# Gated cross-attention block with a mixture of experts: the dense second layer as three bf16 products

## The reference

```python
x = x + tanh(g_xattn[0]) * xattn(layernorm(x), ctx, ctx, wq, wk, wv)   # 16 heads of depth 8, 77 keys
x = x + tanh(g_ffn[0])   * ffn(layernorm(x), Wr, br, W1, b1, W2, b2)

def ffn(x, ...):                       # E = 8 experts, the best K = 2 for each row, H = 256
    logits = x @ Wr + br
    gates  = softmax(where(in_top_2(logits), logits, -inf))
    h      = relu(einsum('btd,edh->bteh', x, W1) + b1)
    return einsum('bte,bteh,ehd->btd', gates, h, W2) + einsum('bte,ed->btd', gates, b2)
```

## Time and profile before

| what | us |
|---|---|
| median of 3 runs | 648.16 |
| lowest and highest of them | 643.82, 649.1 |
| the profiled execution: span from the first to the last instruction | 693.9 |
| PE busy in it | 579.1 (83%) |
| DVE busy | 374.7 (54%) |
| ACT busy | 363.7 (52%) |
| POOL busy | 265.3 (38%) |

### The profile page before, as it was taken

How to read it: one execution, slowest core, us unless ns; L and a number is a source line. 1 busy time by engine, 2 the same in 40 slices (tenths; PEclk the granted TensorE clock), 3 DMA queues, 4 the chain that set the end, 5 groups by cost and what they waited for, 6 DMA issues and landing times.

```text
span 693.9 us, 18476 instructions
## 1 busy us (share of the span) xinstructions
PE 579.1 (83%) x6201; PEld 412.4 (59%) x6213; DVE 374.7 (54%) x1361; ACT 363.7 (52%) x835; POOL 265.3 (38%) x281
## 2 busy tenths in 40 slices
PE   2459998989787999899789899788886788899877
PEld 0225555555455566666467667466664587778656
DVE  4455876688655765445765554665543331242354
ACT  5216765655455466666456656455555345456222
POOL 6020010100554002443544435544455255566660
PEclk9968998988788899999999999899999689999999
DMA  4445644544433376664676654553332245764221
GB/s 116 118 115 148 159 107 126 137 105 119 142 95 112 73 118 104 148 103 138 104 132 115 147 109 139 97 125 83 97 107 81 70 98 136 133 148 128 77 77 49
DMA packets 158121, 78.65 MB, mean 113 GB/s; under 512 B 85088, under 2 KB 153312, under 8 KB 158032
## 3 DMA queue, kind: packets, MB, share of 16 engines
q1 hardware_dynamic: 119760, 45.65, 30.4%
q0 software_dynamic: 7168, 14.69, 8.9%
q10 hardware_dynamic: 31104, 17.13, 8.9%
HBM read 30.72 MB, written 36.75 MB: 97 GB/s over the span
## 4 chain that ended last, share of the span: by engine, by line
PE 65%; issue 9%; DMA 7%; DVE 7%; ACT 7%; another core or an unknown queue 2%; POOL 1%; ACTq 1%; SPq 1%; DVEq 0%; POOLq 0%
PE y L607 11%; PE bank_oT L517 9%; PE scores L503 8%; PE max_scores L482 5%; DMA q_st<-q_dram 4%; PE hidden_p L591 4%; PE o L530 3%; PE hidden_p L592 3%; PE hidden_p L593 3%; DVE neg_max L1028 3%; ACT probs L744 2%; PE max_scores L541 2%; PE bank_oT L648 2%; ACT hidden L810 2%
## 5 line engine op out<-in xcount | busy, mean ns | idle before, releaser
L1028 DVE TENSOR_REDUCE neg_max<-max_scores 128x4 f32<-128x308 f32 x244 | 116.2, 476 | 158.7 <-PE max_scores L482 149.4
L744 ACT ACTIVATE probs<-scores 77x512 f32<-77x512 f32 x256 | 148.8, 596 | 69.9 <-PE scores L503 64.2
L1351 POOL DMA_INDIRECT xs_dram<-rows,at x112 | 110.1, 983 | 92.6 <-PE max_scores L482 57.4
L1366 POOL DMA_INDIRECT back<-ys_dram,at x112 | 107.8, 963 | 90.4 <-PE max_scores L482 35.9
L517 PE MATMUL bank_oT<-probs,v_cols 77*9 77x128 f32 x2048 | 110.0, 291 | 13.6 <-ACT probs L744 8.6
L503 PE MATMUL scores<-q_st,k_st 128*77 128x128 bf16 x1024 | 111.7, 236 | 0.1
L482 PE MATMUL max_scores<-k_st,q_st 128*128 128x308 bf16 x244 | 78.8, 323 | 34.9 <-DVE neg_max L1028 12.3
L503 PEld LDWEIGHTS scores<-q_st,k_st 128*77 128x77 bf16 x1024 | 76.5, 124 | 50.8 <-issue 43.7
L810 ACT ACTIVATE hidden<-hidden_p,b_cols 128x128 f32<-128x128 f32 x256 | 73.5, 369 | 54.3 <-PE hidden_p L593 43.3
L607 PE MATMUL y<-w_sb,hidden 128*128 x608 | 96.8, 299 | 0.0
L607 PEld LDWEIGHTS y<-w_sb,hidden 128*128 128x128 f32 x608 | 84.7, 201 | 2.7
(11 more groups left out here) (144 smaller groups left out, 931.9 us busy)
## 6 DMA issues: line engine op xcount, KB each, us to landing
ys_dram<-ys ACTq DMA_DIRECT2D x38, 256.0 KB
q_st<-q_dram SPq DMA_DIRECT2D x16, 512.0 KB
k_st<-k_dram SPq DMA_DIRECT2D x64, 77.0 KB
xs_all<-x SPq DMA_DIRECT2D x16, 256.0 KB, 4.2
q_dram<-q_hl SPq DMA_DIRECT2D x16, 256.0 KB
xs_dram<-zeros_b ACTq DMA_DIRECT2D x16, 256.0 KB, 3.5
out<-xs_all SPq DMA_DIRECT2D x16, 256.0 KB
k_dram<-k_hl SPq DMA_DIRECT2D x48, 77.0 KB
```

Of the source, the lines that this page charges most:

```text
L744: nc.scalar.activation(probs[h][:], score_bank[h % 2][0:KEYS, :], ACT.Exp, scale=SCALE).then_inc(s_exp, 1)
L1028: V.tensor_reduce(neg_max[:, i // 2, :, h, i % 2], max_to(b, h)[:, 0:PER * KEYS].rearrange("p (j k) -> p j k", j=PER), AXIS_X, ALU.max, ne ...
L1351: G.indirect_dma_start(out=xs_dram[c % 2], out_offset=bass.IndirectOffsetOnAxis(ap=at[k][c % 4][:, i:i + 1], axis=0), in_=rows[c % 2][:, i ...
L1366: G.indirect_dma_start(out=back[k][:, b % 16, :], out_offset=None, in_=ys_dram[c % 2][0:TILES[c] * 128, :], in_offset=bass.IndirectOffsetO ...
```

## The change

In the dense second layer the two f32 matmuls of each sequence become six bf16 matmuls: for each chunk of units, high half by high half of the weights, high half by low half, and low half by high half. The high half of the units is the `upper` view of `dense_hidden`; the low halves are written by DVE into `dense_low`, which lies over two of the key tiles. The halves of the weights, `w2_hi` and `w2_lo`, are made once by POOL in slots 31 and 33.

```diff
         w2_sb = sb("w2_sb", [128, E * HC * D])
+        w2_hi = sb("w2_hi", [128, E * HC * D], BF16)
+        w2_lo = sb("w2_lo", [128, E * HC * D], BF16)
...
+        dense_low = [k_st[i][:].rearrange("p h i j k -> p (h i j k)")[:, 0:HC * WIDE].rearrange("p (m n) -> p m n", m=HC)
+                     for i in range(2)]
...
@@ tensor: dense_out(n)
                 pe.wait_ge(s_drelu, HC * (n + 1))
+                pe.wait_ge(s_dlow, HC * (n + 1))
                 if n == 0:
+                    pe.wait_ge(s_w2lo, 2)
                     pe.wait_ge(s_oT, B)
...
                     mm(o, ones_b[:], b2_split[:, e * HID:e * HID + D], start=True, stop=False, skip_group_check=True)
                     for m in range(HC):
-                        last = mm(o, dense_hidden[n % 2][:, m, i * S:(i + 1) * S],
-                                  w2_sb[:, (e * HC + m) * D:(e * HC + m + 1) * D], start=False, stop=(m == HC - 1),
-                                  skip_group_check=True)
+                        w = slice((e * HC + m) * D, (e * HC + m + 1) * D)
+                        high = upper(dense_hidden[n % 2][:, m, i * S:(i + 1) * S])
+                        mm(o, high, w2_hi[:, w], start=False, stop=False, skip_group_check=True)
+                        mm(o, high, w2_lo[:, w], start=False, stop=False, skip_group_check=True)
+                        last = mm(o, dense_low[n % 2][:, m, i * S:(i + 1) * S], w2_hi[:, w], start=False,
+                                  stop=(m == HC - 1), skip_group_check=True)
                 last.then_inc(p_dy, 1)
...
@@ vector: new function, and its place in slot(t)
+            def dense_hidden_low(n):
+                for m in range(HC):
+                    dve.wait_ge(s_drelu, HC * n + m + 1)
+                    if n >= 2:
+                        dve.wait_ge(p_dy, n - 1)
+                    V.tensor_tensor(dense_low[n % 2][:, m, :], dense_hidden[n % 2][:, m, :],
+                                    upper(dense_hidden[n % 2][:, m, :]), ALU.subtract).then_inc(s_dlow, 1)
...
                 for n in dense_at(t - 1):
                     dense_add(n)
+                for n in dense_at(t):
+                    dense_hidden_low(n)
...
@@ gpsimd: new function, and its place in slot(t)
+            def split_second(part):
+                half = slice(part * (E * HC * D // 2), (part + 1) * (E * HC * D // 2))
+                pool.wait_ge(s_w, 16 * 8)
+                G.tensor_copy(w2_hi[:, half], upper(w2_sb[:])[:, half]).then_inc(s_w2hi, 1)
+                pool.wait_ge(s_w2hi, part + 1)
+                G.tensor_tensor(w2_lo[:, half], w2_sb[:, half], w2_hi[:, half], ALU.subtract).then_inc(s_w2lo, 1)
...
+                if t in (31, 33):
+                    split_second((t - 31) // 2)
                 if r == 0 and group_on(u - 1):
                     rstd1_of(u - 1)
```

More of the change, by code:

```diff
@@ L255, in flamingo_kernel @@
         s_wlo, s_b2s = sem("w1_lo_made"), sem("b2_split_step")
+        s_w2hi, s_w2lo, s_dlow = sem("w2_hi_made"), sem("w2_lo_made"), sem("dense_hidden_low_made")
         s_tanh = sem("tanh_made")
```

## The result

The changed kernel takes 663.34 us (median of 4 runs, 660.17 to 666.0), the kernel before on the same chip 647.32 (4 runs): a ratio of 1.025, 95% interval 1.020 to 1.031. It is slower by about 16 us. The forecast was 651.8 with a range up to 661.0, so the time lies above the range. Times are medians of all executions; the ratios leave out executions over 1.5% above the fastest of their kernel, and every ratio is against the kernel before on the same chip.

The account below looks back on a forecast made before the run. PE was taken as the bound in the two-slot steps, POOL's gathers and DVE's queue in the end: 5.9 lost there, 3.35 regained, 1.0 for held gathers, +3.6 on 648.16, so 651.8 us, range 645.0 to 661.0.

Parts of the forecast that it names:

- the halves of the weights: POOL's split in slots 31 and 33: hidden by POOL's idle time; DVE held 0 to 2 us, taken as 0.
- The products: Dense second layer on PE: bf16 matmuls 0.056 us apart, a sequence 0.39, 10.7 us less PE work in all.
- PE's gain ahead of slot 92: Steps 0 to 4: low halves hidden, PE keeps 0.67 us each, so slot 92 starts 3.35 earlier.
- The chain: Steps 6 to 15: out, additions, low halves, next out in series; a step takes 4.24 us against 3.53.
- The end before: Unchanged kernel, slot 92 to last additions: 45.0 us, with the last gather used 4.67 after its start.
- The end after: Changed kernel, slot 92 to last additions: 50.9 us, 5.9 more than before, plus 1.0 for held gathers.
- the ports: DVE's low halves hold about 7 gathers of slots 92 to 97 by 0.15 each: last group 1.0 us later.
- the sum of 3.6: Whole change: the end loses 5.9, 3.35 come back, +2.6 us; with 1.0 for held gathers +3.6.
- rival 2: Clock falls in the end, PE working 67%: 667.5 us with all ten steps, 659.7 with five; chance 0.17.
- rival 3: Twelve low halves beside gathers of slots 92 to 97 hold POOL 0.68 each, 8.2 us: 659.0; chance 0.06.
- Rival 1: Faster: low halves come before PE needs them, so PE keeps the whole gain: 637.5 us; chance 0.06.
- rival 4: The bf16 products don't come at 0.056 us, so an out stays at 2.24: 657.8; chance 0.05.

Follow-up runs that it names:

- the kernel before once more: The kernel before, unchanged, run again for a second, undisturbed profile: 645.79 us.
- the run with the halves moved, the low halves first and late sums: Changed kernel with weight split in slots 47 and 49, low halves ahead of DVE's additions, late gathers' additions five slots behind instead of two: 643.87 us, ratio 0.995.

## Why the prediction was wrong

**The step that failed** is "DVE operations beside it may be held as POOL's were: 0 to 2 us, I take 0", on the halves of the weights. Measured by themselves they cost 7.6 us, and moving them took 8.5 off the change (6.6 by the ratios), which brings it into the range. They were called hidden by POOL's idle time of the earlier trace rows, which is true of POOL and says nothing of DVE. In slots 31 and 33 DVE has routing operations with two inputs in SBUF, which were held by 5.0 us in all; `head_max` waits behind them and PE behind that, for 3.29 us in slot 31. The lower clock after PE's stands adds to it; how much is not shown. None of the rivals had this mechanism.

**The products** were right: 0.39 per sequence. PE's gain ahead of slot 92 was there and somewhat smaller than forecast: from the first addition of step 0 to that of step 5 are five steps, and they take 55.1 to 55.6 us in the three undisturbed profiles with the f32 products there (604.88 - 549.25 = 55.63 in the kernel before once more) and 52.5 to 53.0 in the eight with bf16 (607.73 - 554.80 = 52.93 in the change). That is 2.6 between the means where 3.35 was forecast. In the times it is lost in the noise: the run without low halves, which has this gain and an end as long as before, takes 653.13, the one with the weights' halves alone 653.23, and each interval is about 3 us to either side.

**The chain** was right: steps of 4.2, and 8.3 us between the runs with and without it once the gathers are out of the way.

**The end before** was 42.4 instead of 45.0: the 4.67 from a gather's start to its use came out of a disturbed execution and is 2.49, which makes 2.2 of the 2.6; the rest is mostly the gathers' pace, 25.2 us for 20 instead of 25.6. That the earlier trace rows belong to the one execution was right, but the same care was not taken with the earlier trace rows.

**The end after** was 54.5 instead of 51.9 with the ports. The last gather is used 36.7 us after the start of slot 92, where the sum had 35.7 + 1.0; that these agree is luck. Inside it the fourth gather of slot 92 began 0.6 later than forecast, the gathers were held more (20 of them take 636.59 - 608.47 = 28.1 instead of the forecast 26.6), and the last is usable 2.1 sooner. What follows took 17.8 instead of 15.2, and those 2.6 are put down to the clock: the additions of the last four steps begin at 640.45, 645.97, 650.18 and 655.79, and the two steps whose out runs mostly at the level of 1.2 GHz take 5.52 and 5.61 instead of 4.21, 2.7 more together. That part is read from the profile; no run took it away with all else equal.

So the sum of 3.6 lacks 7.6 for the weights' halves, 2.6 for the end before and 2.6 for the end after, which makes 16.4; measured are 16.0 between the medians. With an interval of 12.7 to 19.8 and a gain ahead of slot 92 that was 0.7 too large in the sum, an agreement this close is chance.

**The rivals.** The fall of the clock (rival 2) came, but not as the rival had it: in the steps, with PE busy for 24.60 and 23.37 of 32 us, the clock is 1.00. It came where PE stood longer, behind the last gathers and ahead of the last out, and for two outs. The port (rival 3) held one gather in three, mostly by 0.4, which makes 2.9 us for 20 gathers and not 8.2. Rival 1 did not come: PE stood 1.17 in such a step. Nor did rival 4: a sequence takes 0.39.

## What to carry to other kernels

Work put into the idle time of one engine can hold another: before calling an operation of POOL hidden, look at what DVE has in the same microseconds, which of it has two inputs in SBUF, and who waits behind that. A stage that a DMA chain ends does not become shorter when its busiest engine gets faster; move the waits for that chain out of the queue, then add up every engine's step anew, since the next bound may be at the same length (3.54 of DVE for 3.53 of PE). And check a duration that carries a sum in a second execution if the first shows stands that nothing explains.

## What the runs showed that was not expected

A gather that is held by a pair of low halves ends at one of two distances behind that pair, about 0.22 or 0.83 us. In the end of the change it is always the second: one of 617.95 + 1.35 = 619.30 behind 618.47. In the run with the halves moved, the low halves first and late sums both occur: 600.07 + 1.28 = 601.35 behind a pair that ends at 601.13, and 607.94 + 1.88 = 609.82 behind one that ends at 608.99, though both gathers begin 0.23 after their pair. So the 0.4 of the change is one case between 0 and 0.93; what decides between the two distances no run shows.

An operation of POOL can hold a DVE operation until it is over, and holds others not at all: beside the subtraction of slot 33 `neg_max`, which reads PSUM, took 0.47 as always, while `rows`, with both inputs in SBUF, took 2.14 instead of 0.68.
